# TensorE's pauses in the preparation stage filled with products that nobody reads

## The reference

```
xn = layernorm(x)
static = xn @ W.T                      # and k = q = rmsnorm(xn per head of 8) * k_norm_w
per step of 512:  S = lam*S;  S += beta * k (x) (-static - k^T S);  o = q^T S     # 16 heads of 8
x = x + layernorm(static + o)*w + b + ffn(xn)       # ffn: silu gate, 128->512, gelu, gelu, ->128
xn = layernorm(x)
x = x + causal_decayed_attention(xn; Wq, Wk, Wv, Wo, gamma) + xn @ W.T + b + (xn @ V) @ C.T
```

## Time and profile before

| what | value |
|---|---|
| median of 3 runs | 791.06 us (790.12 to 791.97) |
| profiled execution, its own time | 785.81 us |
| its span, first to last instruction | 784.1 us |
| mean granted clock of TensorE in the span | 0.985 |
| busy: PE, DVE, ACT, POOL | 712.4, 726.6, 587.3, 645.4 us |
| the preparation, first instruction to the first one behind the join | 0 to 142.0 us |
| recurrence and first feed-forward | 142 to about 536 us |

### The profile page before, as it was taken

One profiled execution on the slowest core, in us unless ns is written; L12 is line 12 of the kernel. 1 busy time (PEld: TensorE's weight loads), 2 busy tenths in 40 slices (PEclk: granted clock), 3 DMA queues, 4 the chain that ended last, 5 costly groups with the idle time before them and its releaser, 6 DMA issues.

```text
span 784.1 us, 13111 instructions
## 1 busy us (share of the span) xinstructions
PE 712.4 (91%) x3349; PEld 513.9 (66%) x3349; DVE 726.6 (93%) x2036; ACT 587.3 (75%) x1363; POOL 645.4 (82%) x640
## 2 busy tenths in 40 slices
PE   4888886599999999999999999777699999999998
PEld 3434343478888888888888888643356666666655
DVE  5999999899999999999999999996789898899987
ACT  6888886689898888889988898764665556657631
POOL 3787889797888979979898898767799789989873
PEclk9999999899999999999999999997999999999999
DMA  5677865501613325171161241501622212120001
GB/s 128 207 261 247 274 223 202 144 15 30 133 40 81 81 61 113 41 147 41 42 146 41 59 89 56 156 26 34 187 82 82 68 41 68 54 70 27 1 27 41
DMA packets 139241, 75.75 MB, mean 97 GB/s; under 512 B 74922, under 2 KB 123052, under 8 KB 139180
## 3 DMA queue, kind: packets, MB, share of 16 engines
q1 hardware_dynamic: 138124, 74.58, 34.4%
q10 hardware_dynamic: 1056, 0.52, 0.2%
HBM read 39.86 MB, written 33.55 MB: 94 GB/s over the span
## 4 chain that ended last, share of the span: by engine, by line
DVE 47%; PE 27%; issue 3%; ACT 2%; POOL 2%; DVEq 0%; POOLq 0%; ACTq 0%; SPq 0%
DVE r_rec L1271 11%; DVE r_gain L1283 9%; DVE r_pg L1257 9%; DVE r_kw L1277 9%; PE f_ps L2429 7%; PE f_ps L2430 6%; DVE r_rec L1291 6%; PE f_ps L2406 5%; DVE l_qs L1345 2%; PE r_rec L2464 1%; PE r_rec L2458 1%; PE r_rec L2448 1%; PE f_ps L2437 1%; PE r_rec L2446 1%; PE f_ps L2397 1%
## 5 line engine op out<-in xcount | busy, mean ns | idle before, releaser
L1672 POOL TENSOR_TENSOR l_kv<-l_qkv 128x1024 f32<-128x1024 f32 x64 | 124.5, 1950 | 18.3 <-PE f_ps L2430 16.6
L1271 DVE TENSOR_REDUCE r_rec<-r_pg 128x32 f32<-128x288 f32 x256 | 129.3, 505 | 0.6 <-ACT r_pg L1891 0.6
L1283 DVE TENSOR_REDUCE r_gain<-r_kw 128x64 f32<-128x256 f32 x256 | 118.7, 464 | 0.0
L1345 DVE TENSOR_TENSOR l_qs<-f_ps,l_qd 128x1024 f32<-128x1024 f32 x64 | 78.1, 1221 | 26.7 <-PE f_ps L2430 19.7
L1542 POOL TENSOR_TENSOR f_hl<-f_h,f_hh 128x512 fp32r<-128x512 f32 x64 | 80.9, 1298 | 24.7 <-ACT f_hh L1937 24.3
L2293 PE MATMUL f_ps<-f_gh,w_hi 128*128 128x512 f32 x256 | 100.0, 391 | 0.9 <-POOL f_gl L1542 0.7
L2293 PE MATMUL f_ps<-f_hh,w_hi 128*128 128x512 f32 x256 | 99.8, 390 | 0.0
L1550 POOL TENSOR_TENSOR f_g<-f_a,f_b 128x512 f32<-128x512 f32 x64 | 82.3, 1297 | 16.3 <-ACT f_b L1926 16.1
L1291 DVE SCALAR_TENSOR_TENSOR r_rec<-r_rec,lam,r_gain 128x64 f32<-128x64 f32 x256 | 86.6, 338 | 0.4 <-ACT r_w L1902 0.3
L1542 POOL TENSOR_TENSOR f_gl<-f_g,f_gh 128x512 fp32r<-128x512 f32 x64 | 82.6, 1304 | 0.0
L1352 DVE TENSOR_REDUCE l_o_in<-l_qs 128x128 f32<-128x1024 f32 x64 | 77.2, 1211 | 0.5
(11 more groups left out here) (229 smaller groups left out, 2088.1 us busy)
## 6 DMA issues: line engine op xcount, KB each, us to landing
scratch_xnT<-p_xnT SPq DMA_DIRECT2D x16, 256.0 KB, 2.9
scratch_K<-p_kout SPq DMA_DIRECT2D x16, 256.0 KB, 2.3
scratch_fac<-p_fac SPq DMA_DIRECT2D x16, 256.0 KB, 2.3
scratch_R<-p_rr SPq DMA_DIRECT2D x16, 256.0 KB, 2.3
scratch_P<-p_pp SPq DMA_DIRECT2D x16, 256.0 KB, 3.0
first_x<-scratch_xnT SPq DMA_DIRECT2D x16, 256.0 KB, 3.6
first_xt<-in_L_attn_x_dram SPq DMA_DIRECT2D x16, 256.0 KB, 2.9
scratch_W<-r_w SPq DMA_DIRECT2D x16, 256.0 KB, 4.2
```

The lines of the kernel that those rows point to most:

```text
L1271: dve.tensor_reduce(w_here(g, blk), pg[q][:, at, :, :, :].rearrange("p (v g) i k -> p v g i k", g=G)[:, :, g, :, :], AX.X, ALU.add).then_i ...
L1283: dve.tensor_reduce(of_group(g, gain), of_group(g, kw), AX.X, ALU.add).then_inc(gain_ok, 1)
L1672: pool.tensor_tensor(dst, k, v, ALU.mult).then_inc(kv_ok, 1)
```

## The change

Three sets of products that nobody reads are added to PE's list in `prepare`, and the helper takes the bank as an argument. In turns 2 to 16, behind `factors` and ahead of `weights`, PE waits until ACT has copied `static` of this turn out of `ps_s`, and then makes 6 products into that bank. In turn 17 it waits for the same sign and makes 20, ahead of the last sequence's `couplings`. Behind the loop it makes 24 into `ps_k`, between the third and the fourth transpose of the largest values.

```diff
-                def unread_products(n):
+                def unread_products(n, bank):
                     for _ in range(n):
-                        nc.tensor.matmul(ps_n[:, 0, 0:P], c.head_ones[:, :], c.ident[:, :], start=True, stop=True)
+                        nc.tensor.matmul(bank[:, 0, 0:P], c.head_ones[:, :], c.ident[:, :], start=True, stop=True)
...
                     if k == 2:
-                        unread_products(12)
+                        unread_products(12, ps_n)
...
                     at(of(k - 3), factors)
                     if k == B + 1:
+                        pe.wait_ge(r_in, B + 1)
+                        unread_products(20, ps_s)
                         couplings(of(B - 1))
+                    if 2 <= k <= B:
+                        pe.wait_ge(r_in, of(k - 2).count(1, 2))
+                        unread_products(6, ps_s)
                     if 0 <= k - 2 < NG:
                         weights(k - 2)
...
                 for n in range(PEAKS):
+                    if n == PEAKS - 1:
+                        unread_products(24, ps_k)
                     pe.wait_ge(peak_done, n + 1)
                     ins = nc.tensor.transpose(ps_x[0:1, n, :], peak[:, n:n + 1], c.ident[:, :])
```

## The result

The changed kernel takes 796.31 us (median of 8 runs, 794.70 to 797.92), the kernel before 790.89 (8 runs, 788.71 to 793.34): ratio 1.0061, interval 1.0044 to 1.0078. It is slower, by 5.4 us where 9.2 were forecast. The time lies in the range of 795 to 803, but outside the likeliest case's own 798.5 to 802.5; of the numbers worked out ahead, rival 1's 795.0 is the nearest.

What follows compares the result with a forecast made beforehand. DVE was taken to bound the preparation, until six products made PE's loop the bound. Couplings 6.6 us late, 8.66 after turn 17, then the end: +9.2 us on the median 791.06 gives 800.3 us, range 795 to 803.

Steps and rivals of the forecast that it cites:

- the likeliest case: Whole kernel: the worked sum, 800.3 us, together with a longer loop; range 798.5 to 802.5, chance 0.76.
- rival 1: Preparation: the clock falls in unprofiled runs; if the products save all 5.25 us, 795.0 us; chance 0.10.
- The bound: Preparation: DVE's turn of 7.66 us, with a loop through PE and ACT 0.1 us shorter.
- The sum of the loop: Turns with weights: copy, wake-up, six products, weights and static make 8.02 us where DVE needs 7.66.
- a product: PE: each unread product takes 0.225 us at 2.4 GHz, so six take 1.35 us.
- Turn 17: Twenty products ahead of the last couplings: 8.61 us from couplings to couplings where 6.53 are needed.
- the end: Twenty-four products ahead of the fourth transpose: DVE's flag ends at 150.68, the next stage starts at 151.3.
- the clock behind the join: Behind the join: a held clock gains 0 us, bounds 0 to 2, as DVE is busy all the time.
- added to their median: Whole kernel: +9.2 us from the profiled execution put on the runs' median of 791.06, giving 800.3 us.
- Hidden products (2): Turns and pauses: products are hidden and the clock pays, so the kernel is faster, 787 us; chance 0.04.
- Only the ends (3): Turns cost nothing; only turn 17 (2.1 us) and the last flag (about 0.5) remain: 793.7 us; chance 0.06.
- A longer loop (4): Turns: some step 0.1 us longer in each of 15 turns, +1.5, 801.8 us; chance shared in the likeliest 0.76.

Runs made afterwards that it cites:

- r3: Changed kernel with only the twenty-four products ahead of the fourth transpose, the other two sets taken out: 791.36 us, ratio 1.0001 to the kernel before.
- r2: Changed kernel with only the twenty products in turn 17, the other two sets taken out: 792.11 us, ratio 1.0025 to the kernel before.
- r6: Kernel before plus only 10 products in turn 17 and 15 at the end, none in turns 2 to 16: 791.75 us, ratio 1.0022.
- r4: Changed kernel with 3 products in turns 3 to 16, 10 in turn 17, 15 at the end: 788.50 us, ratio 0.9957 to the kernel before.
- r7: Changed kernel with 12 products in place of 6 in turns 2 to 16: 816.63 us (2 runs).
- r1: Changed kernel with only the six products in turns 2 to 16, the other two sets taken out: 796.43 us, ratio 1.0073 to the kernel before.
- r5: Kernel before plus only 3 products in turns 3 to 16, none in turn 17 or at the end: 789.17 us, ratio 0.9985.
- r11: r4 profiled once more, with 3, 10 and 15 products: join at 142.37, no time given.

## Why the prediction came out as it did

*What was right.* The bound: the preparation is set by DVE with a second loop through PE and ACT 0.2 us shorter (7.45 for 7.66; 0.1 was read), and filling PE's pause makes that loop the bound. The sum of the loop was 8.02, measured 7.96; a product 0.225, measured 0.223. Turn 17 cost 8.36 from couplings to couplings (8.61), the end came out within 0.4 us. The join moved by 9.2 us between the two first profiles, which hides a fall of 1.5 us in turn 2 of the changed kernel; in its second profile, which has none, the join comes 8.2 us later than in the first of before, just under the 8.6 to 9.5 stated. So the products' own cost was put about 1 us too high. That the clock behind the join is worth nothing for the time was not contradicted: with it lost there, the rest of the span took 641.9 to 645.0 us in four profiles of the kernel before and 646.0 in one of the changed kernel, with it kept over the join 643.0 in the other (both fall again from 160 to 166 us), and r3, which adds only the products ahead of the join, has the ratio 1.0001. A gain beyond that spread isn't seen; a smaller one isn't excluded.

*The step that failed* is the one from the profiled execution to the median: "added to their median", the +9.2 was put on runs 5.25 us slower than the execution from which it was worked out, with the clock in the turns priced at 0. The sum lacked a term, the clock that the products save. It is rival 1 of the prediction, which got 0.10 and whose 795.0 us is nearer to the 796.31 measured than the 800.3 is. Its price for a slow turn, 1.8 us, was 9.09 - 7.65 = 1.44 in the fourth profile, of which the next turns win some back. The time is in the range because the range reached down to this rival. The runs show the term: three further profiles of the kernel before have 2, 2 and 3 falls ahead of the join, single profiles of three kernels with its turns (r2, r6, r3) 1, 4 and 6, and only its first profile none. Neither of the changed kernel's profiles has one between 25 us and the join, and three products in place of six, which cost the turns nothing, make the kernel faster than before (r4). Fourteen stretches at 1.00 were taken for a property of the kernel; they were one draw, and the 5.25 us were the sign of it.

*The size of the missing term.* The mean join of the four profiles of before is (142.17 + 144.02 + 144.05 + 144.37) / 4 = 143.65, that of the two of the changed kernel 150.89: +7.2 where 9.2 were forecast. Of these 2.0 us, 1.5 are the later joins of before (143.65 for 142.17), which is the clock; the other 0.5 is what the changed kernel's joins lie under the forecast. The times say more: 9.2 - 5.4 = 3.8. Most of what lies between is which executions the profiles caught. The span and the mean granted clock of each timed execution are on record. The four profiled spans of before (784.1, 785.9, 789.0, 787.7) have the mean 786.7, where the 58 timed ones have the median 789.2; the two of the changed kernel have 795.4, where its eight have 794.6. And the span goes with the clock: 21 of the 58 have a granted clock of 0.970 or less and spans of 791.2 on average, 13 have 0.982 or more and 786.7. The four profiles have 0.985, 0.979, 0.976 and 0.980, so none is of the slowest third; r3, with six falls, has 0.974. The changed kernel has 0.980 to 0.991. Where the slowest third loses its clock, in the turns or behind the join, no trace shows: from the join to the end of the span the kernel before took 641.9, 641.9, 645.0 and 643.3 us in its four profiles, so there too executions differ by 3 us.

*The other rivals.* Hidden products (2): refuted by r7 for six, true for three. Only the ends (3): refuted by the turns of 7.96 us; r1 shows that the six are most of the slowdown (4.7 us of span, 5.4 for the whole change). A longer loop (4): no, 0.06 us shorter.

*Of the change itself:* its three sets did not fit their pauses, 6 where 3 fit, 20 where 10 fit or nearly fit, 24 where 15 fit. What it is for is real: r4 with about half the products keeps the clock and costs nothing in the turns.

The Trainium skill ("TensorE: Matmul & The Clock Gate", section "Why this matters for your kernels") advises against idle gaps between bursts of matmuls, since they put the clock back. The traces agree for the pause of turn 17, 3.24 us long, in five profiles of the seven that leave it open. In the turns they show falls beside pauses of 1.06 to 1.54 us, shorter than the gaps that the page's row names, so those falls stand by the traces alone.

## What to carry to other kernels

Work that nobody reads is free only up to the slack of the loop in which it stands, not up to the length of the pause that one sees: put down what the next wait behind it would be (here the factors' sign, 0.9 us behind the copy), and count that. If the profiled execution is faster than all the timed runs, as 785.81 us was with 790.12 to 791.97, don't add a difference worked out in it to their median: take more profiles, or price what differs between them first. And see what a new wait hangs on in every turn: in turn 17 the same copy was late by a store.

## What the runs showed of the hardware

The granted clock fell to 0.50 in some executions and not in others of the same kernel, with PE's longest pauses in the turns at 1.06 to 1.54 us, and while PE was counted busy in the very stretch. A fall lengthened the couplings from 1.54 to 2.90 us and a turn with weights from 7.65 to about 9.0. With three products more in each turn, no fall came in the turns of three profiles (r4, r5, r11); with ten or twenty in the pause of turn 17, none came there in seven. Over the 58 timed executions of the kernel before, those with a granted clock of 0.970 or less were 4.5 us longer on average than those with 0.982 or more.
